# Fillers ahead of the two head loops of a decoder kernel: 32-row tiled 32-bit matmuls in place of full-array bf16 ones

## The reference

```
x = ln(x + attn0(x))       # 16 heads, 2 x 8 features each, rotary, softmax(a1) - lam * softmax(a2)
x = ln(x + xattn0(x, ctx)) # one head of 128
x = ln(x + ffn0(x))        # top 1 of 8 experts, 128 -> 512 -> 128
x = ln(x + attn1(x))       # 16 heads of 8 features, causal
x = ln(x + xattn1(x, ctx)) # 16 heads of 64
x = ln(x + ffn1(x))        # top 4 of 16 experts, 128 -> 256 -> 128
```

## Time and profile before

| | |
|---|---|
| median of 3 runs | 569.14 us |
| the runs | 554.63, 570.70, 569.14 us |
| profiled execution, first to last instruction | 567.3 us |
| PE busy | 503.6 us, 4127 matmul records |
| PE weight loads busy | 365.9 us |
| DVE, ACT, POOL busy | 288.8, 236.0, 123.0 us |
| mean granted PE clock | 0.898 of full |

### The profile page before, as it was taken

One profiled execution on the slowest core, in us unless ns is written; L12 is line 12 of the kernel. 1 busy time (PEld: TensorE's weight loads), 2 busy tenths in 40 slices (PEclk: granted clock), 3 DMA queues, 4 the chain that ended last, 5 costly groups with the idle time before them and its releaser, 6 DMA issues.

```text
span 567.3 us, 11138 instructions
## 1 busy us (share of the span) xinstructions
PE 503.6 (89%) x4127; PEld 365.9 (65%) x4128; DVE 288.8 (51%) x690; ACT 236.0 (42%) x418; POOL 123.0 (22%) x233
## 2 busy tenths in 40 slices
PE   7678999998769998499986899999988999999994
PEld 3436887776443994257663677777777667777774
DVE  3945455663684437155516866666634343333336
ACT  1523444674230523014552466666660543333330
POOL 5622322451310022221205222222221000000001
PEclk9875555899978999859997999999999999999999
DMA  8665233303030001553001000001000011111110
GB/s 211 199 200 153 87 99 100 110 27 149 1 149 0 2 2 33 154 148 113 8 25 38 12 13 13 13 13 48 1 2 1 19 30 39 37 37 37 37 28 37
DMA packets 23129, 34.37 MB, mean 61 GB/s; under 512 B 7680, under 2 KB 15824, under 8 KB 22832
## 3 DMA queue, kind: packets, MB, share of 16 engines
q1 hardware_dynamic: 23088, 33.81, 20.1%
HBM read 28.26 MB, written 5.24 MB: 59 GB/s over the span
## 4 chain that ended last, share of the span: by engine, by line
PE 73%; DVE 14%; DMA 5%; ACT 4%; issue 2%; POOL 1%; SPq 0%; POOLq 0%; DVEq 0%; ACTq 0%
PE ps L1000 10%; PE ps L983 10%; PE ps L632 6%; PE ps L610 5%; PE ps L597 5%; PE ps L899 5%; PE ps L872 3%; PE ps L971 3%; PE ps L644 2%; PE ps L880 2%; PE ps L888 2%; PE ps L586 2%; PE ps L807 2%; PE ps L594 2%; PE ps L841 2%
## 5 line engine op out<-in xcount | busy, mean ns | idle before, releaser
L1326 DVE TENSOR_REDUCE negm<-ps 128x4 f32<-128x512 f32 x96 | 64.1, 688 | 69.8 <-PE ps L597 68.0
L1048 ACT ACTIVATE probs<-ps 128x512 f32<-128x512 f32 (+1 forms) x100 | 56.5, 592 | 30.6 <-PE ps L610 29.8
L1653 DVE SCALAR_TENSOR_TENSOR racc<-ps,sm,racc 128x128 f32<-128x128 f32 x128 | 36.0, 344 | 63.1 <-PE ps L1000 63.0
L1048 ACT ACTIVATE arena<-ps,w1a 128x512 f32<-128x512 f32 x64 | 43.4, 687 | 59.0 <-PE ps L983 57.8
L1000 PEld LDWEIGHTS ps<-w1a,arena 128*128 128x128 f32 x512 | 59.4, 192 | 7.2 <-issue 6.2
L1000 PE MATMUL ps<-w1a,arena 128*128 128x128 f32 x512 | 59.8, 275 | 0.8 <-DVE racc L1644 0.8
L983 PE MATMUL ps<-xT,w1a 128*128 128x512 f32 x128 | 57.9, 594 | 1.4 <-ACT xT L1048 1.4
L1048 ACT ACTIVATE arena<-ps 128x512 f32<-128x512 f32 (+4 forms) x62 | 35.1, 574 | 43.2 <-PE ps L807 15.9
L565 POOL TENSOR_TENSOR probs<-probs,rzE 128x480 f32<-128x480 f32 x32 | 30.6, 988 | 76.0 <-DVE rzE L1591 76.0
L586 PE MATMUL ps<-onesb 128*128 128x512 bf16 x134 | 37.0, 435 | 7.6 <-ACT vall L1048 4.5
L517 POOL TENSOR_SCALAR rstd<-mv 128x4 f32<-128x4 f32 x12 | 2.7, 228 | 182.8 <-DVE mv L1372 182.8
(11 more groups left out here) (198 smaller groups left out, 894.8 us busy)
## 6 DMA issues: line engine op xcount, KB each, us to landing
stackA<-arena SPq DMA_DIRECT2D x12, 256.0 KB, 2.8
arena<-stackA SPq DMA_DIRECT2D x24, 96.0 KB
arena<-stackA SPq DMA_DIRECT2D x8, 288.0 KB
w1a<-in_w1a SPq DMA_DIRECT2D x1, 2048.0 KB, 7.7
w2a<-in_w2a SPq DMA_DIRECT2D x1, 2048.0 KB, 7.5
w1a<-in_w1b SPq DMA_DIRECT2D x16, 128.0 KB, 2.1
w1a<-in_w2b SPq DMA_DIRECT2D x16, 128.0 KB, 2.0
stackD<-arena SPq DMA_DIRECT2D x6, 256.0 KB
```

The lines of the kernel that those rows point to most:

```text
L1048: return nc.scalar.activation(o, i, f, **kw)
L1326: nc.vector.tensor_reduce(negm[:, slot % 2, 4 * g:4 * g + 4], tiles(bank(BANK_S + g % 2), 4, P), AX.X, ALU.max, negate=True).then_inc(a.ma ...
L1653: last = stt(racc[:, b, :], bank(banks + half)[:, k * P:(k + 1) * P], sm[:, 11, bass.ds(b * E1 + e, 1)], racc[:, b, :], ALU.mult, ALU.add)
```

## The change

POOL fills one more tile, `onesr`, 128x128 of type float32r, with ones, as the ninth memset at the start; the later counts of `fixed` go up by one. A new function issues matmuls on 32 rows each (32 rows by 128 columns of weights, 128 moving columns), the quadrants in turn, with the output of quadrant q in bank q:

```diff
@@ block.sync, heads
-                sp.wait_ge(fixed, 3 if count == NH else 10)
+                sp.wait_ge(fixed, 3 if count == NH else 11)
@@ block.gpsimd
-                    (vs[:, :, :, :, 16:17], 1.0))):
+                    (vs[:, :, :, :, 16:17], 1.0), (onesr[:].bitcast(F32), 1.0))):
                 nc.gpsimd.memset(tile, value).then_inc(fixed, 1)
                 pool.wait_ge(fixed, n + 1)
...
-            pool.wait_ge(fixed, 9)
+            pool.wait_ge(fixed, 10)
             nc.gpsimd.memset(ones_late, ONES_PAIR).then_inc(fixed, 1)
-            pool.wait_ge(fixed, 10)
+            pool.wait_ge(fixed, 11)
@@ block.tensor
+            def keep_rows_busy(rounds, quadrants, tile):
+
+                for n in range(rounds):
+                    for q in quadrants:
+                        rows = slice(32 * q, 32 * q + 32)
+                        mm(bank(q)[:, n % 4 * P:(n % 4 + 1) * P], tile[rows, 0:P], tile[rows, 0:P], start=True, stop=True)
...
             pe.wait_ge(fixed, 8)
-            keep_busy(26, BANK_M0)
+            pe.wait_ge(ld_c, 16)
+            pe.wait_ge(fixed, 9)
+            keep_rows_busy(14, range(4), con)
+            keep_rows_busy(24, range(4), onesr)
...
-            keep_busy(40, BANK_M0)
+            keep_rows_busy(16, range(2), onesr)
+            keep_rows_busy(16, range(2), con)
+            keep_busy(20, BANK_M0)
             pe.wait_ge(D.vall, 2)
             pe.wait_ge(D.full, 2)
             heads(D, PAIRS, pair=True, causal=True)
```

More of the change, by code:

```diff
@@ L17 @@
 F32 = mybir.dt.float32
+F32R = mybir.dt.float32r
 BF16 = mybir.dt.bfloat16
@@ L115, in decoder_kernel @@
         identb, trib, onesb, causS, causT = (sb(n, [P, P], BF16) for n in ("identb", "trib", "onesb", "causS", "causT"))
+        onesr = sb("onesr", [P, P], F32R)
         one = sb("one", [P, 1])
```

## The result

| | runs | median us | lowest to highest |
|---|---|---|---|
| before | 4 | 565.0 | 554.63 to 570.70 |
| changed | 4 | 568.28 | 564.87 to 571.04 |
| before, shared by three later series | 51 | 564.6 | 552.2 to 588.2 |
| changed, run again | 6 | 561.48 | 556.46 to 591.28 |

The ratio of the first comparison is 1.0183 (1.0125 to 1.0242), that of the repetition 1.0031 (0.9951 to 1.0111). Medians and ranges in this text count every run, ratios only those within 1.5% of a kernel's fastest, which leaves two of before in the first comparison, 554.63 and 560.85, and is why it looks like 2%. Over all runs the change makes no difference that can be told from the spread: the mean is 569.0 us over 10 runs of the changed kernel (standard deviation 11.4) and 565.6 over the 51 of before (8.6), a difference of 3.4 with an error of 3.8.

The account below looks back on a forecast made before the run. PE's speed was taken to bound the kernel, mainly loop A's low-clock stretch, about 21 us. The median 569.1 plus 0.2 for A, nothing for D and a little for the rest gave 570 us, own range 564 to 576, wider 551 to 596.

Parts of the forecast that it names:

- What bounds the kernel: Whole kernel: PE's speed counts; loop A's low-clock stretch, some 7.5 turns at 2.79 us extra, costs about 21 us.
- Price of a record: Fillers ahead of A and D: side by side, 63 ns a record at the low clock and 36 at the full one.
- rival 2: Ahead of A: row strips' weight loads queue; about 575 at full clock (0.12), 594 to 600 at low clock (0.12).
- `onesr` is one pass: New fillers: one record per matmul, priced in a queue as bf16, 107 ns at the low clock and 54 at full.
- The start of A is 0.2 us late: Ahead of A: fillers take 9.7 us, the loop starts 1.6 later, 1.4 of it covered; cost 0.2 us.
- so a start up to 1.4 us later costs nothing: Start of A: the `mT` DMA took 3.65 us, the next 2.27, so 1.4 us of delay is covered.
- D costs nothing: Ahead of D: fillers take 10.3 us where 8.8 stood, end at 234.1, stack lands at 239.75; cost nothing.
- The low-clock case I had as a worst one: Ahead of D: if the clock falls within the fillers, they end at about 246, 6 us late.
- the held clock: Ahead of D: queued loads end fillers at 236.7, the clock might stay full; worth at most 8 us.
- The low stretch comes back about where it did: Loop A: the clock returns to full near 103.8 us, as before, after turns of 6.75 us.
- two rivals: Loop A: low stretch ends early or doesn't come, 549 or 555 (0.21); or lasts longer, 581 or 593 (0.15).
- New fillers don't thicken it: Start of loop A: PE is busy only about half of 39 to 42 us; fillers ahead leave this thin start unchanged.

Follow-up runs that it names:

- Moving the first packet away: Changed kernel with PE's first fillers, at 1 us, cut from 9 of 512 columns into 36 of 128; 555.8 us in one run.
- D part only: Changed kernel with the old 26 fillers back ahead of A, the new ones kept ahead of D; median 560.9 us, ratio to before 0.999.
- thick start: Full-array fillers added inside loop starts: kernel before, A 557.4 us, A and D 551.2, with still more fillers 549.2; changed kernel, A only 570.4 (medians).
- one-strip fillers: Changed kernel with all row-tiled fillers ahead of A on quadrant 0 and bank 0, same matmuls and counts; 622.5 us in one run.
- 40 wide ones: Changed kernel with row-tiled fillers ahead of A of 512 (a few 256) moving columns, 40 matmuls in place of 152; median 562.6 us, ratio to before 1.003.
- 104 narrow ones: Kernel before with its 26 full-array fillers of 512 columns ahead of A cut into 104 of 128; median 567.1 us, ratio to before 0.994.

## Why the prediction was right

The forecast was 570, between 551 and 596, and no change; measured 568.28 and 561.48, with no difference to be told. It was right in the total and in the reason for the width, and wrong in steps whose errors the spread covers. That 568.28 lies so near to 570 is luck: the forecast stood on 569.14, the median of three runs, and over 51 runs the kernel before has 564.6.

- **What bounds the kernel**: right. The low stretch of loop A is the large item, and the spread of before is of its kind (the clock row has four slices at 5, not three). The line above confirms it with 0.38 us per low microsecond; loop A's own 2.79 of 6.75 us is 0.41.
- **Price of a record**: right side, sizes off. I took 63 and 36 ns from the value product; measured are 53 at the low clock (213 / 4) and 30 at the full one. The fillers ahead of A took 8.2 us and not 9.7, so their part of the sum was zero as forecast, with 1.5 us less. Those ahead of D took 10.0 us in the repetition's profile, where the clock stayed full (forecast 10.3), and 13.3 in the first, where it fell: a record on two strips costs about 56 ns at the full clock and 104 at the low one. The queue of weight loads (rival 2) doesn't exist across strips. Within one strip a record takes 213 ns, the bound that the prediction had for a queue; whether the load alone sets that isn't shown.
- **`onesr` is one pass**: wrong. It leaves one record per matmul, but that record costs on one strip what an f32 record costs, and not the bf16 matmul's 107 ns. Side by side it doesn't matter.
- **The start of A is 0.2 us late**: wrong, 4.6 in this profile. The step that failed is "so a start up to 1.4 us later costs nothing", with the `mT` DMA as the gate: the gate was the store and the first stack load before it, and I counted no cost for the instructions themselves. Two fetch packets met DMAs on which the start hangs: the store took 3.79 us and not 2.14, the first query load 5.99 where those without a packet took 4.0 to 4.4. Moving the first packet away gave a store of 2.14 us again and the first scores at 38.99. The 1.4 us of cover was too simple as well: the `mT` DMA took 3.31 to 5.91 us in the chains, and with the old fillers and no packet the turns began up to 3.1 us late (D part only). Not all of the 4.6 us is the packets'.
- **D costs nothing**: right. The low-clock case I had as a worst one happened (the clock fell in the two-strip fillers), they ended at 240.0 and not at 246, and still were in time since the stack came at 242.6. The clock then rose in the last 20 fillers, was full for the first 0.8 us of the loop, and came back 3.7 us sooner than before: -2.8 us here. That isn't the held clock for which I had given a gain to the queue, and it is chance: D as a whole gained nothing in the other profiles.
- **"The low stretch comes back about where it did"**: right in the first profile, 103.5 against 103.8, and by chance. In the other profiles without a thick start it ended between 56 and 107, and at 175.8 with one-strip fillers. By the prediction's own last sign, a changed count of low turns in loop A, it failed at the repetition: the clock was back at 79.8 after a first value product at 57.05, some 3.4 low turns in place of 7.5. This should have been the prediction's centre: not one time with two rivals, but a spread of 554 to 590 in both kernels.
- **"New fillers don't thicken it"**: right, and shown by its reverse: work inside both starts changed the runs, other fillers ahead of them or none hardly did.

What stays open: why the clock rises when it does in turns that are alike, and what decides the falls that a thick start leaves: the one at 71 follows a late `mT` DMA, the one at 57 a wait that two other profiles stood. The Trainium skill, "TensorE: Matmul & The Clock Gate", Part 1, has activity of PE release the clock; with 57.65 of 60 us busy at 0.50, and 44 us of one-strip fillers at 0.50, these rows don't agree with taking a busy PE for that activity. What of a turn raises the clock wasn't tried.

## What to carry to other kernels

Fillers have to stand where PE is thin, in the first turns of a loop and up to the landing of what it waits for; ahead of it they warm a clock that falls again. A kernel whose clock can stay low for a whole loop needs ten or more runs before two per cent mean anything (an estimate from the deviation of 8.6 us over 51 runs), and its runs are best compared at equal low time. A gain that one profile shows in one stage may be where its clock happened to change: look for it in the profiles of the other kernels with the same stage. Added instructions are not free even in idle time: their fetch can land in a DMA that gates the next stage. Fewer and wider ones are no sure way out (40 wide ones still met the store, 104 narrow ones missed it), so look at the instruction queue's packets when a DMA takes 2 us longer than before.

## What was not expected of the hardware

- A 16 KB packet of the instruction queue inside a 256 KB store makes it last 3.6 to 4.4 us (five profiles) and not 2.13 to 2.16 (the nine others); in the changed kernel the 16 DMA engines together are 5% busy for 1.2 us of it.
- Four 32-row strips with 128 weight columns of a 32-bit type overlap fully, weight loads too: about 53 ns a record at 1.2 GHz against 213 on one strip and 104 on two.
- A float32r record on 32 x 128 costs the same 213 ns as an f32 one at that clock.
- One strip busy without a break for 44 us left the clock at 1.2 GHz. In two-strip fillers it fell in three of seven profiles (near 229.8 in the first) and stayed full in the other four. It rose in the four-strip ones ahead of loop A (0.50 at 31 to 34, 1.00 at 36.2 to 38.4), as it does in full-array bf16.
